# A two-block graph-attention kernel: a new opening, a reordered attention in block 1, and eight one-hots moved to GpSimd

## The reference

```python
def gat_conv(x, src, dst, W, a_src, a_dst, b, heads, out_ch):   # self-loops already appended
    h = (x @ W).reshape(n, heads, out_ch)
    alpha_src = jnp.einsum('nhc,hc->nh', h, a_src)
    alpha_dst = jnp.einsum('nhc,hc->nh', h, a_dst)
    e = jax.nn.leaky_relu(alpha_src[src] + alpha_dst[dst], 0.2)
    p = jnp.exp(e - segment_max(e, dst)[dst])
    alpha = p / segment_sum(p, dst)[dst]
    return segment_sum(h[src] * alpha, dst) + b

# block 0 (L0): 8 heads of 768, then one of 768
h = jax.nn.elu(gat_conv(x, src, dst, W1, a_src1, a_dst1, b1, 8, 768))
x = _layernorm(x + gat_conv(h, src, dst, W2, a_src2, a_dst2, b2, 1, 768))
# block 1 (L1): 4 heads of 256, then one of 768
h  = relu(layer_norm(gat_conv(x, W1, ..., 4, 256), g1, be1)) + (x @ Wr1 + br1)
h2 = layer_norm(gat_conv(h, W2, ..., 1, 768), g2, be2) + (h @ Wr2 + br2)
x = _layernorm(x + h2)
```

## Time and profile before

| | |
|---|---|
| median of three runs | 365.04 us |
| the profiled execution | 364.43 us |
| its span, first to last instruction | 362.6 us |
| TensorE busy | 349.9 us, 96% |
| GpSimd, ScalarE, VectorE busy | 67%, 60%, 59% |
| DMA | 65.15 MB, mean 180 GB/s |

### The profile page before, as it was taken

One profiled execution on the slowest core, in us unless ns is written; L12 is line 12 of the kernel. 1 busy time (PEld: TensorE's weight loads), 2 busy tenths in 40 slices (PEclk: granted clock), 3 DMA queues, 4 the chain that ended last, 5 costly groups with the idle time before them and its releaser, 6 DMA issues.

```text
span 362.6 us, 6075 instructions
## 1 busy us (share of the span) xinstructions
PE 349.9 (96%) x2058; PEld 299.1 (82%) x2060; DVE 213.9 (59%) x544; ACT 218.5 (60%) x375; POOL 242.5 (67%) x163
## 2 busy tenths in 40 slices
PE   8999899999999999999999999999999999999994
PEld 4888788888988988988898898898677787788883
DVE  4998864445427327344542832637687767953776
ACT  4995668646745854764775585475476667264601
POOL 2389648784793965779479396574258589687911
PEclk9999999999999999999999999999999999999999
DMA  7988948566646547555664764666072654437002
GB/s 234 302 297 238 398 163 252 183 179 171 198 155 222 163 140 243 162 193 174 174 194 156 217 169 141 251 167 223 5 248 95 209 153 123 161 104 240 6 2 87
DMA packets 24544, 65.15 MB, mean 180 GB/s; under 512 B 1952, under 2 KB 3024, under 8 KB 24528
## 3 DMA queue, kind: packets, MB, share of 16 engines
q1 hardware_dynamic: 20864, 55.02, 46.0%
q10 hardware_dynamic: 3664, 9.92, 10.4%
HBM read 64.15 MB, written 0.79 MB: 179 GB/s over the span
## 4 chain that ended last, share of the span: by engine, by line
PE 78%; DVE 12%; ACT 6%; DMA 2%; issue 1%; ACTq 0%; DVEq 0%
PE ps L985 57%; PE ps L1070 8%; PE ps L1274 5%; PE ps L1104 2%; ACT e L757 1%; DMA b_rows<-in_L_gnn_b 1%; PE ps L1049 1%; DVE e L1491 1%; DVE ps L1544 1%; PE ps L1166 1%; DMA raw<-in_L_gnn_W 1%; ACT ring_hi L357 1%; DVE ps L1554 1%; DVE ps L1628 1%; PE ps L1338 1%
## 5 line engine op out<-in xcount | busy, mean ns | idle before, releaser
L370 POOL TENSOR_TENSOR ring_lo<-raw,ring_hi 128x768 fp32r<-128x768 f32 x92 | 167.0, 1854 | 74.6 <-ACT ring_hi L357 74.6
L357 ACT ACTIVATE ring_hi<-raw 128x768 fp32r<-128x768 f32 x96 | 77.3, 840 | 34.9 <-PE ps L985 28.9
L386 POOL TENSOR_TENSOR ring_lo<-raw,ring_hi 128x512 fp32r<-128x512 f32 (+1 forms) x40 | 59.5, 1519 | 22.5 <-ACT ring_hi L379 22.4
L985 PE MATMUL ps<-ring_hi,zT_hi 128*128 128x256 f32 (+1 forms) x256 | 69.3, 346 | 0.7 <-ACT zT_hi L799 0.7
L985 PE MATMUL ps<-ring_lo,zT_hi 128*128 128x256 f32 (+1 forms) x256 | 67.1, 337 | 0.0
L985 PE MATMUL ps<-ring_hi,zT_lo 128*128 128x256 f32 (+1 forms) x256 | 66.8, 338 | 0.0
L1491 DVE CUSTOM_DVE_ANT_0 e<-ps,att 128x768 f32<-128x768 f32 x38 | 34.3, 957 | 47.5 <-PE ps L985 47.5
L985 PE MATMUL ps<-ring_hi,xT_hi 128*128 128x512 f32 x192 | 51.2, 342 | 0.0
L985 PE MATMUL ps<-ring_lo,xT_hi 128*128 128x512 f32 x192 | 50.0, 336 | 0.0
L985 PE MATMUL ps<-ring_hi,xT_lo 128*128 128x512 f32 x192 | 49.8, 337 | 0.0
L985 PEld LDWEIGHTS ps<-ring_lo,zT_hi 128*128 128x128 f32 x256 | 43.0, 188 | 5.7
(11 more groups left out here) (172 smaller groups left out, 546.9 us busy)
## 6 DMA issues: line engine op xcount, KB each, us to landing
raw<-in_L_gnn_W SPq DMA_DIRECT2D x54, 768.0 KB, 4.5
raw<-in_L_gnn_Wr SPq DMA_DIRECT2D x8, 768.0 KB, 4.3
att<-in_L_gnn_a_src ACTq DMA_DIRECT2D x10, 384.0 KB, 4.0
att<-in_L_gnn_a_dst ACTq DMA_DIRECT2D x10, 384.0 KB, 5.4
raw<-in_L_gnn_W SPq DMA_DIRECT2D x4, 384.0 KB, 5.2
x_sb<-in_x SPq DMA_DIRECT2D x3, 256.0 KB, 5.1
rows_hc<-in_L_gnn_b SPq DMA_DIRECT2D x1, 512.0 KB, 7.9
rows_hc<-in_L_gnn_g SPq DMA_DIRECT2D x1, 512.0 KB, 8.7
```

Source lines behind the costliest of these rows:

```text
L357: eng.activation(slot_hi(c), raw_chunk(c), ACT.Copy).then_inc(hi_done, 1)
L370: eng.tensor_tensor(slot_lo(c), raw_chunk(c), slot_hi(c).bitcast(F32), ALU.subtract)\
L386: eng.tensor_tensor(ring_lo[:, q["ring_at"]:q["ring_at"] + w], raw[:, q["raw_group"], q["raw_at"]:q["raw_at"] + w], ring_hi[:, q["ring_at" ...
L985: last = pe.matmul(ps[:, at + to:at + to + hi - lo], a, b[:, lo:hi], start=start and n == 0 and to != D, stop=stop and n == PASSES - 1, sk ...
```

## The change

Four edits.

**Opening.** SP no longer loads the first third of x and the edges; ACT issues these three DMAs as its first instructions. The edges come as 64 rows of 128 (`edge_rows`), are cast, transposed by TensorE into PSUM and copied to `edges_f`, so that edge 128t+p is in partition p (an order of its own for the counting). The first third of x is rounded in two pieces of one 128-column chunk each, and TensorE starts chunk 0 on the first; it runs the three passes of chunks 0 and 2 one after the other, and waits for `ring_lo` ahead of the second pass only. The two `keep_warm` products behind the first transposes go.

**Counting.** GpSimd makes the one-hots 0 to 7, DVE the other 24.

**Heads 0 and 1.** `far` is made in two halves; ACT copies the step sums ahead of two splits; head 1's first h_hi goes between the pieces of ELU 0, its scores and leaky branch come earlier.

**Block 1.** `leaks` of half A goes ahead of its second h_hi; DVE masks and weighs half A ahead of the dots of half B; `leaks` and `exps` of half B go ahead of the DMAs for the next attention vectors.

```diff
@@ the opening, SP and GpSimd @@
             sp.dma_start(raw[:, 0, 0:D], w1[:, 0, 0, :]).then_inc(single_loaded[0], 16)
-            load_x(0)
-            sp.dma_start(edges[:, 0, :], src.rearrange("(p t) -> p t", p=P)).then_inc(edges_loaded, 16)
-            sp.dma_start(edges[:, 1, :], dst.rearrange("(p t) -> p t", p=P)).then_inc(edges_loaded, 16)
             sp.dma_start(raw[:, 0, D:2 * D], w1[:, 1, 0, :]).then_inc(raw_full[0], 16)
-            load_x(1)
+            load_x(sp, 1)
...
+            pool.wait_ge(iota_cast, 1)
+            pool.wait_ge(edges_split, 4)
+            for t in range(POOL_HOTS):
+                pool.tensor_scalar(hot(t), iota[:, 1:1 + P], row_of[:, t:t + 1], weight_of[:, t:t + 1], ALU.is_equal,
+                                   ALU.mult).then_inc(hot_pool_done, 1)
             for c in range(FIRST, POOL_CH):
                 split_lo(pool, FIRST_PHASE, c)
@@ ScalarE @@
+            load_x(act, 0)
+            act.dma_start(edge_rows[0:ET, :], src.rearrange("(t p) -> t p", p=P)).then_inc(edges_loaded, 16)
+            act.dma_start(edge_rows[ET:2 * ET, :], dst.rearrange("(t p) -> t p", p=P)).then_inc(edges_loaded, 16)
             act.wait_ge(half_set, 1)
...
             split_hi(act, FIRST_PHASE, 0, reused=False)
             act.dma_start(b1_rows[:, :], b0_b1.rearrange("(t p) -> t p", p=P)).then_inc(b1_loaded, 16)
-            input_hi(0)
+            input_hi(0, 1, 1)
+            input_hi(1, 1, 2)
             split_hi(act, FIRST_PHASE, 1, reused=False)
...
             leaks(0)
+            act.wait_ge(counted, 1)
+            act.activation(step_sums, ps[:, STEPS_AT:STEPS_AT + 1 + N], ACT.Copy).then_inc(sums_copied, 1)
             att_for(1)
             for c in (0, 1):
                 split_hi(act, 2, c)
-            act.wait_ge(counted, 1)
-            act.activation(step_sums, ps[:, STEPS_AT:STEPS_AT + 1 + N], ACT.Copy).then_inc(sums_copied, 1)
-            act.wait_ge(far_done, 1)
+            act.wait_ge(far_done, NT)
...
-            elu(0)
+            elu(0, between=lambda: projected_after_dots(1, 0))
+            leaks(1)
             split_hi(act, 2, 4)
+            projected_after_dots(1, 1)
+            exps(1, (1, 0))
             split_hi(act, 2, 5)
-            softmax_and_elu(1)
+            after_exps(1)
...
             x1_scale(1)
+            leaks(A_GAT1A)
             features_hi(A_GAT1A, tiles=(1,))
             chunks_hi(14, 15)
-            leaks(A_GAT1A)
             exps(A_GAT1A, (0, 1))
+            chunks_hi(15, 19)
             features_hi(A_GAT1B, tiles=(0,))
-            chunks_hi(15, 18)
+            chunks_hi(19, 21)
             features_hi(A_GAT1B, tiles=(1,))
             weights_hi(A_GAT1A)
-            chunks_hi(18, 21)
+            leaks(A_GAT1B)
+            exps(A_GAT1B, (0, 1))
...
@@ TensorE @@
             transpose_x(0)
-            keep_warm(2, PROJ + 2 * BANK)
...
                 if c in (0, 2):
-                    pe.wait_ge(xT_hi_done, c // 2 + 1)
-                    chunk(FIRST_PHASE, c)
-                    for passes in (FIRST_TWO, LAST_ONE):
+                    pe.wait_ge(xT_hi_done, c + 1)
+                    pe.wait_ge(hi_done, c + 1)
+                    for passes in ((0,), (1,), LAST_ONE):
+                        if passes == (1,):
+                            chunk(FIRST_PHASE, c)
                         if passes is LAST_ONE:
                             pe.wait_ge(xT_lo_done, c // 2 + 1)
+                        if passes is LAST_ONE and c == 0:
+                            pe.wait_ge(edges_cast, 1)
+                            pe.wait_ge(iota_cast, 2)
+                            pe.transpose(ps[:, EDGES_AT:EDGES_AT + 2 * ET], edge_rows_f[:, :],
+                                         ident[0:2 * ET, 0:2 * ET]).then_inc(edges_ps, 1)
...
             def rest_of_head(h, scores_at=1, first=0):
                 for c in range(first, CH):
                     if c == scores_at:
-                        pe.wait_ge(z_lo_done, 3 * h)
+                        pe.wait_ge(z_lo_done, 3 * h - 1 if first else 3 * h)
@@ VectorE @@
             split_lo(dve, FIRST_PHASE, 0)
+            dve.wait_ge(edges_loaded, 32)
+            dve.tensor_copy(edge_rows_f[:, :], edge_rows[:, :]).then_inc(edges_cast, 1)
             input_lo(0)
-            dve.wait_ge(edges_loaded, 32)
-            dve.tensor_copy(edges_f[:, :, :], edges[:, :, :]).then_inc(edges_cast, 1)
-            dve.wait_ge(edges_cast, 1)
+            dve.wait_ge(edges_ps, 1)
+            dve.tensor_copy(edges_f[:, :, :].rearrange("p s t -> p (s t)"), ps[:, EDGES_AT:EDGES_AT + 2 * ET])\
+               .then_inc(edges_placed, 1)
+            dve.wait_ge(edges_placed, 1)
...
-            hots(0, ET)
+            hots(POOL_HOTS, ET)
```

More of the change, by code:

```diff
@@ L139, in build_gnn @@
         iota = sb("iota", [P, 1 + N], BF16)
-        edges = sb("edges", [P, 2, ET], I32)
+        edge_rows = sb("edge_rows", [2 * ET, P], I32)
+        edge_rows_f = sb("edge_rows_f", [2 * ET, P])
         edges_f = sb("edges_f", [P, 2, ET])
@@ L460, in masked_at @@
                 return am_at(a, i)
-            at = s_at(a, k) + (2 * BANK if i == 0 else 0)
+            at = s_at(a, k)
+            if i == 0:
+                at = 5 * BANK + k * N if a == A_GAT1A else at + 2 * BANK
             return ps[:, at:at + N]
@@ L527, in three, with load_x @@
             return ((hi_a, hi_b), (hi_a, lo_b), (lo_a, hi_b))
+        def load_x(eng, b):
+            cols = slice(2 * b * P, (2 * b + 2) * P)
+            eng.dma_start(x_sb[:, :, cols], x.rearrange("(t p) c -> p t c", p=P)[:, :, cols])\
+               .then_inc(x_loaded[b], 16)
         @block.sync
@@ L696, in steps, with input_hi @@
                     act.activation(step(t), iota[:, :], ACT.Sign, bias=src_bias[:, t:t + 1]).then_inc(step_act_done, 1)
-            def input_hi(b):
-                act.wait_ge(xT_ps, b + 1)
-                act.activation(xT_hi[:, 2 * b:2 * b + 2, :].rearrange("p k n -> p (k n)"),
-                               ps[:, XT_AT + b * BANK:XT_AT + (b + 1) * BANK], ACT.Copy).then_inc(xT_hi_done, 1)
+            def input_hi(first, chunks, at_done):
+                act.wait_ge(xT_ps, at_done)
+                act.activation(xT_hi[:, first:first + chunks, :].rearrange("p k n -> p (k n)"),
+                               ps[:, XT_AT[first]:XT_AT[first] + chunks * N], ACT.Copy).then_inc(xT_hi_done, 1)
             split_hi(act, FIRST_PHASE, 0, reused=False)
             act.dma_start(b1_rows[:, :], b0_b1.rearrange("(t p) -> t p", p=P)).then_inc(b1_loaded, 16)
-            input_hi(0)
+            input_hi(0, 1, 1)
+            input_hi(1, 1, 2)
             split_hi(act, FIRST_PHASE, 1, reused=False)
@@ L728, in projected_hi, with projected_after_dots @@
                     projected_tile_hi(h, i)
+            def projected_after_dots(h, i):
+                act.wait_ge(a_dst_done, 2 * h + 2)
+                projected_tile_hi(h, i)
             def projected_tile_hi(h, i):
@@ L778, in weights_tiles_hi, with elu @@
                     act.activation(*weights_tile(a, pT_hi, i), ACT.Copy).then_inc(wt_hi_done, 1)
-            def elu(h):
+            def elu(h, between=None):
                 for q in range(3):
@@ L793, in elu @@
                     act.activation(pair, pair, ACT.Exp, scale=-1.0).then_inc(elu_exp, 1)
+                if between is not None:
+                    between()
                 elu_hi(h, 2)
@@ L812, in softmax_and_elu, with after_exps @@
                 exps(h, (1, 0))
+                after_exps(h, last)
+            def after_exps(h, last=False):
                 att_for(h + 1, last)
@@ L931, in _ @@
                    .then_inc(att_loaded, 16)
-            leaks(A_GAT1B)
-            exps(A_GAT1B, (0, 1))
             residual_scale(0, 0)
@@ L1040, in weights @@
                 if is_gat1(a):
+                    pe.wait_ge(h_lo1_done, 2 * late(a) + 2)
                     pe.wait_ge(p_done, before(a) + 2 * HH)
@@ L1127, in transpose_x @@
                 pe.wait_ge(x_loaded[b], 16)
+                if b == 2:
+                    pe.wait_ge(xT_lo_done, 1)
                 for k in (2 * b, 2 * b + 1):
                     for i in range(NT):
-                        at = XT_AT + k * N + i * P
+                        at = XT_AT[k] + i * P
                         last = pe.transpose(ps[:, at:at + P], x_sb[:, i, k * P:(k + 1) * P], ident[:, :])
-                last.then_inc(xT_ps, 1)
+                    if b == 0 or k % 2 == 1:
+                        last.then_inc(xT_ps, 1)
             transpose_x(0)
-            keep_warm(2, PROJ + 2 * BANK)
             for c in range(CH):
@@ L1160, in count_edges @@
                 for t in range(ET):
-                    pe.wait_ge(hot_done, t + 1)
+                    if t < POOL_HOTS:
+                        pe.wait_ge(hot_pool_done, t + 1)
+                    else:
+                        pe.wait_ge(hot_done, t + 1 - POOL_HOTS)
```

(16 more changed lines are left out.)

36 lines of the change are left out of this document (19 added, 17 removed).

## The result

The changed kernel takes 369.77 us (median of 4 runs, 368.54 to 370.76) against 364.96 us: ratio 1.0124, 95% interval 1.0105 to 1.0142. It is 4.8 us slower, where 364.0 us, 1.0 us faster, was forecast. The profiled execution has a span of 367.0 us against 362.6.

The account below looks back on a forecast made before the run. TensorE, busy 96% of the span, was taken as the bound, other engines counting only where it waits. Attention -3.0 and opening +2.0 gave -1.0: 364.0 us, range 361.7 to 365.5 with the rivals.

Parts of the forecast that it names:

- Head 1, the step that failed: Split moved behind head 1's exponentials: its ring_lo ready at 56.9, wanted at 57.1, so hidden with 0.2 us to spare.
- GpSimd's one-hots: Eight one-hots on GpSimd during the opening, 0.4 us each, 3.2 us in all, hidden; VectorE gains 2.6 us.
- The opening: Bias DMA held behind the 768 KB load, landing at 11.4, so chunk 1 starts 2.0 us later.
- rival 1: In the opening, the bias is not held up: 0 to 0.3 us gained there, 361.9 us in total; chance 0.27.
- Head 0: Step sums copied ahead of two splits and VectorE freed earlier: 0.6 us won at head 0's wait at 38.25.
- Head 1's chain up to its weights: Earlier scores and leaky branch bring VectorE's chain to head 1's weights 0.5 us forward, 56.5 for 57.00.
- Block 1: TensorE's waits at the weights of halves A and B both go: 1.2 + 0.7 = 1.9 us won.
- Rival 2: TensorE's clock falls in the opening's new wait for the bias: 1.8 us added, 365.8 us; chance 0.08.
- The sum: Over the whole kernel, -3.0 for the attention and +2.0 for the opening give -1.0 us.
- the attention: Heads 0 and 1 and block 1 together: -0.6 - 0.5 - 1.9 = -3.0 us.
- the forecast's own range: Whole kernel, 363.3 to 364.9 us: opening at +1.4 to +2.6, attention at -2.5 to -3.1.

Follow-up runs that it names:

- e3: The changed kernel with all one-hots on VectorE and the split of chunk 5 ahead of head 1's exponentials again: 365.98 us, ratio 1.0026.
- e6: The changed kernel with all one-hots on VectorE and two late splits moved from ahead of head 1's ELU to ahead of its last third: 361.99 us, 0.9920.
- e9: The kernel before the change with the new opening alone: 365.90 us against 365.21, ratio 1.0016.
- e4: e3 with the bias DMA issued behind the edges' at ScalarE's start: 365.93 us, ratio 1.0023.
- g1: e6 with the bias DMA issued behind the edges' at ScalarE's start: 362.24 us, ratio 0.9928.
- g2: g1 with VectorE's ring_lo of chunks 1 and 2 and ScalarE's split of chunk 2 moved earlier: 361.48 us, ratio 0.9912.
- e7: The kernel before the change with the reordered attention of block 1 alone: 362.74 us, ratio 0.9935.
- e2: The changed kernel with the split of chunk 5 ahead of head 1's exponentials again, one-hots still on GpSimd: 370.63 us, ratio 1.0166.
- e1: The changed kernel with all 32 one-hots on VectorE: 365.70 us, ratio 1.0009 against the kernel before.

## Why the prediction was wrong, by its own steps

**Head 1, the step that failed.** "The split moved behind the exponentials ends at 55.0 and its ring_lo (1.84) at 56.9, TensorE wants it at 57.1: hidden, with 0.2 us to spare." This step failed in what it followed: I asked only when TensorE wants the result. The same ring_lo also frees the raw buffer on which SP waits, the load behind it feeds two splits on ScalarE, and head 1's ELU is queued behind those. Nor did I price the leaky branch put ahead of the other split, which delays that load with the moved split put back too (e3). Priced at nothing, it cost 4.08 us: 2.30 of waiting, about 1.6 of half clock and 0.2 of smaller gaps around the wait. e6 shows that the queueing was the cause.

**GpSimd's one-hots.** I bounded one at 0.31 to 1.25 us and took 0.4, "since it is a quarter of the columns and one input less". It took 1.13, so "hidden" became +2.70, inside the 1.7 to 3.7 that I had worked out for the upper end. The failure is the choice, and a range (up to 365.5) that left that end out. By itself the form takes 0.8; the rest is, by the sum above, the time beside VectorE's subtractions.

**The opening.** +2.0 forecast, +0.93 in the profile, 0.6 to 0.7 in e9. The mechanism fell: the 768 KB load was issued at 3.90, 0.96 ahead of the bias (4.86), yet the bias landed at 10.36, 5.5 us behind its issue (before: 5.3), while that load took 8.2 to 12.1. It was not held behind it, as rival 1 said: from issue to landing the bias took 5.0 to 6.1 us in six profiles with the old opening and 5.1 to 6.0 in seven with the new one. What came later was the issue, behind a split whose weights landed at 4.85 rather than 4.10. That moves from run to run: in the same profiles the issue lies at 4.10 to 4.54 and at 4.17 to 5.10, and the bias row starts at 9.37 to 10.63 and at 9.69 to 10.84. The means differ by 0.3 us, less than either spread.

**Head 0.** -0.6 forecast, -0.72 in the profile. My chain counted on VectorE "freed 2.6 us earlier from the one-hots", and e4, g1 and g2 bear that out: with all one-hots on VectorE and TensorE on time, nothing is gained. But in the changed kernel TensorE was also 3.63 us late at the counting, so that this profile alone doesn't tell the term from luck.

**Head 1's chain up to its weights.** -0.5 forecast, -0.61 in the profile, and -0.60 to -0.63 in every run with the new order: right.

**Block 1.** -1.9 forecast, -2.27 in the profile, -2.4 alone (e7): right, a little small. I took the brackets for the whole gap. In TensorE's timeline of the kernel before, the last matmul ahead of half A's weights starts at 289.23 and such matmuls follow each other by 0.23, so the gap was 290.82 - 289.46 = 1.36 us, not 1.19; at half B, behind 301.96, it was 0.88, not 0.71.

**Rival 2** (the clock falls in a new wait) had the mechanism and nearly its price (1.8 forecast, 1.6 found) but the wrong wait, and a chance of 0.08. It came at head 2, and in the profiles of e2, e7 and e9 behind waits at chunk 4 or at the bias. I let it decide "from a bias that lands later than about 11", after 2.6 us of waiting; in e9 1.45 us went before a fall.

**The sum.** With what the runs measured, +0.9 + 2.7 - 0.7 - 0.6 + 4.1 + 0.3 - 2.3 = +4.4. My -3.0 for the attention was there (-3.6, of which head 0's 0.7 with the reserve above); it was outweighed by two edits that I had priced at nothing. Of the +0.3 between head 2 and block 1 I have no account: it comes behind the weights of head 7, and e2 has it too (+0.31), e1 not. The upper end of the forecast's own range was also summed 0.2 too low: 365.04 + 2.6 - 2.5 is 365.1, not 364.9.
